# A decoder layer on one core: the first normalisation made a tile ahead and turned by VectorE in 32x32 squares, banks dealt anew, and a new order of the last attention step

## What is computed

```python
x = x + _L0_attn_ref(_layernorm(x, axis=-1), L0_attn_W_qkv, L0_attn_W_out, L0_attn_b_out)
x = x + _L0_xattn_ref(_layernorm(x, axis=-1), ctx_1024, ctx_1024, mask_Bx1xSxS2_ik1, ...)
x = x + _L0_ffn_ref(_layernorm(x, axis=-1), L0_ffn_w1, L0_ffn_b1, L0_ffn_w2, L0_ffn_b2)
```

## Time and profile before

| | us |
|---|---|
| median of 3 runs | 1269.24 |
| lowest, highest | 1269.16, 1270.24 |
| the profiled execution's own time | 1269.33 |
| its span, first to last instruction | 1266.9 |
| PE busy in the span | 1250.7 (99%) |
| DVE, ACT, POOL busy | 665.5, 487.4, 244.3 |

### The profile page before, as it was taken

The page is one execution under the profiler, slowest core; times in us unless marked ns, Lnnn a source line. Parts: engine busy times, 40 slices in busy tenths (PEclk is TensorE's granted clock), DMA queues, the critical chain, the costliest instruction groups (busy, mean ns, idle before and its releaser), DMA issues.

```text
span 1266.9 us, 15607 instructions
## 1 busy us (share of the span) xinstructions
PE 1250.7 (99%) x5785; PEld 1039.4 (82%) x5785; DVE 665.5 (53%) x1210; ACT 487.4 (38%) x887; POOL 244.3 (19%) x225
## 2 busy tenths in 40 slices
PE   9989999999999999999999999999999999999998
PEld 7878888888888888867888888888888888888887
DVE  7476858585858585856733443333424334433211
ACT  7246555545454545444332222322222322223221
POOL 2303232323232313138601002001001010020000
PEclk9999999999999999999999999999999999999999
DMA  8210202020202020316210010010100100100000
GB/s 294 81 63 13 76 14 75 13 75 12 75 12 75 12 75 12 125 40 210 75 67 1 1 67 1 1 66 0 36 30 0 66 0 0 66 0 0 34 1 34
DMA packets 40486, 60.04 MB, mean 47 GB/s; under 512 B 4224, under 2 KB 14464, under 8 KB 40448
## 3 DMA queue, kind: packets, MB, share of 16 engines
q1 hardware_dynamic: 40448, 59.53, 14.1%
HBM read 41.17 MB, written 18.35 MB: 47 GB/s over the span
## 4 chain that ended last, share of the span: by engine, by line
PE 54%; DMA 1%; SPq 0%; DVE 0%; ACT 0%; issue 0%; DVEq 0%
PE bank L50 18%; PE bank L52 18%; PE bank L51 18%; DMA w_raw<-in_w 0%; DMA x_dram<-resid 0%; DVE resid L1166 0%; SPq L1049 0%; DVE w_parts L185 0%; ACT w_parts L181 0%; SPq L1047 0%; SPq L189 0%; SPq L1046 0%; DVEq L1165 0%; SPq L1056 0%
## 5 line engine op out<-in xcount | busy, mean ns | idle before, releaser
L1156 DVE TENSOR_TENSOR hid_lo<-gelu_out,hid_hi 128x512 fp32r<-128x512 f32 x128 | 98.2, 767 | 399.1 <-ACT gelu_out L1123 399.0
L50 PE MATMUL bank<-zT,w_parts 128*128 128x512 f32 x768 | 299.3, 390 | 4.9 <-DVE zT L150 1.8
L52 PE MATMUL bank<-zT,w_parts 128*128 128x512 f32 x768 | 298.8, 389 | 0.0
L51 PE MATMUL bank<-zT,w_parts 128*128 128x512 f32 x768 | 298.8, 389 | 0.0
L1119 ACT ACTIVATE hid_hi<-bank,b_col 128x512 fp32r<-128x512 f32 x128 | 88.3, 690 | 491.0 <-PE bank L52 491.0
L50 PE MATMUL bank<-w2p_hi,hid_lo 128*128 128x512 f32 x512 | 199.3, 389 | 0.7 <-DVE hid_lo L1156 0.7
L52 PE MATMUL bank<-w2p_hi,hid_hi 128*128 128x512 f32 x512 | 199.2, 389 | 0.0
L51 PE MATMUL bank<-w2p_lo,hid_hi 128*128 128x512 f32 x512 | 199.2, 389 | 0.0
L50 PEld LDWEIGHTS bank<-zT,w_parts 128*128 128x128 f32 x768 | 144.2, 188 | 36.7 <-issue 3.0
L51 PEld LDWEIGHTS bank<-zT,w_parts 128*128 128x128 f32 x768 | 144.2, 188 | 29.8
L52 PEld LDWEIGHTS bank<-zT,w_parts 128*128 128x128 f32 x768 | 144.0, 188 | 29.9
(11 more groups left out here) (141 smaller groups left out, 1811.0 us busy)
## 6 DMA issues: line engine op xcount, KB each, us to landing
x_in<-in_x SPq DMA_DIRECT2D x32, 256.0 KB, 3.7
x_dram<-resid SPq DMA_DIRECT2D x32, 256.0 KB, 2.1
w_raw<-in_w SPq DMA_DIRECT2D x32, 256.0 KB, 3.4
resid<-x_dram SPq DMA_DIRECT2D x32, 256.0 KB, 3.1
out_dram<-resid SPq DMA_DIRECT2D x32, 256.0 KB, 2.1
resid<-in_wqkvT SPq DMA_DIRECT2D x12, 256.0 KB, 4.8
mask_i<-in_mask SPq DMA_DIRECT2D x16, 128.0 KB, 2.6
values_now<-values_dram SPq DMA_DIRECT2D x8, 256.0 KB, 2.8
```

Of the source, the lines that this page charges most:

```text
L50: pe.matmul(out_ap, lhs[1], rhs[0], start=start, stop=False)
L51: pe.matmul(out_ap, lhs[0], rhs[1], start=False, stop=False)
L52: return pe.matmul(out_ap, lhs[0], rhs[0], start=False, stop=stop)
L1156: dve.tensor_tensor(hid[1][:, c % 4, :], gelu_out[:, c % 2, :], f(hid[0][:, c % 4, :]), ALU.subtract).then_inc(hid_lo, 1)
```

## The change

**z1.** Rows of tile n are now loaded a second time into `ahead` (four buffers laid over `w1_raw` and `w2_raw`), their statistics are made in step n - 2, and in step n - 1 DVE makes the norm rows (`rows_ahead`) and turns them in 16 square transposes (`turn`) into the new `z1_cols`. ACT and DVE then split `z1_cols` into zT at the start of step n (`z1_high`, `z1_low`), as soon as the queries are done. PE's 16 transposes of z1 go from steps 1 to 7; the setup keeps those of tile 0. The norm rows of z1 leave the start of the step.

**Setup.** `load_ahead(1)` adds four transfers of 256 KB; DVE adds four statistics and their aggregation for tile 1 after its splits. The context values now wait in `z1_cols`, so in step 0 the first `turn` waits until they are stored.

**Banks and waits.** The tables are new; y goes to banks 0 to 3, and each chunk of it waits for `q_low` of its bank. The cross scores 0 to 3 wait for each `q_low` singly.

**Last step.** A new order of PE, ACT and DVE, the four `second_residual` of tile 7 moved into the feed-forward stage (before the second `w1_low` there), b1 and b2 loaded at the start of the attention block, and the gelu table loaded by a tiny activation in the last step.

The core of the diff:

```diff
                             if n == RAWS + NB - 1:
                                 for i in range(NB):
                                     load_x(sp, 0, i)
+                                load_ahead(sp, 1)
...
+                        stats_ahead(dve, 1, range(NB))
+                        aggregate(dve, 1, mv1, ln1)
                         dve.wait_ge(bias_loaded, 64)
...
+                        def rows_ahead(n, b):
+                            if b is not None:
+                                dve.wait_ge(z2T_done, NB * (b + 1))
+                            norm_rows(dve, lambda i: ahead[i], mv1, rstd1, ln1, n)
+                            dve.wait_ge(z1_ready, NB * (n + 1))
                             dve.nop(nofuse=True)
...
+                        def turn(a, first_turn, count):
+                            if more(a):
+                                for n in range(first_turn, first_turn + count):
+                                    dve.transpose(*squares(n, z1_cols)).then_inc(z1_turned, 1)
...
-                                for j in range(4):
+                                for j in range(3):
                                     mask_scores(b, j)
+                                if more(a):
+                                    rows_ahead(a + 1, b)
+                                mask_scores(b, 3)
+                            else:
+                                rows_ahead(1, None)
+                                dve.wait_ge(values_stored, 16 * BATCH)
+                                dve.nop(nofuse=True)
+                            turn(a, 0, 3)
                             for m in range(EC):
-                                low(yv, m, 4 + m, y_hi, y_lo, EC * a + m + 1)
-                            for i in range(NB):
+                                low(yv, m, m, y_hi, y_lo, EC * a + m + 1)
+                                if m == 2:
+                                    turn(a, 3, 2)
+                            turn(a, 5, 5)
+                            for i in range(NB):
+                                if i == 2:
+                                    turn(a, 10, 2)
...
+                            turn(a, 12, 2)
                             dve.wait_ge(s1_exp, NB * (a + 1))
...
+                            turn(a, 14, 2)
                             dve.wait_ge(pT_hi, a + 1)
...
-                                second_residual(b, 0, 1 - par)
-                                second_residual(b, 1, 1 - par)
-                                next_stats(dve, a + 1, (2, 3))
-                                second_residual(b, 2, 1 - par)
+                                second_residual(dve, b, 0, 1 - par)
+                                second_residual(dve, b, 1, 1 - par)
+                            if twice_more(a):
+                                stats_ahead(dve, a + 2, (2, 3))
+                                aggregate(dve, a + 2, mv1, ln1)
...
                             if b is not None:
                                 queries(b, range(EC))
-                                transposed_chunks(pe, a, 4)
...
-                            for i in range(NB):
-                                second_residual(b, i, b % 2, LAST_PROJ_BANK)
...
+                            act.wait_ge(b_loaded, 32)
+                            act.activation(gelu_table, b1_col[:, 0:1], ACT.Gelu)
...
+                            if splits_weights(t) and c == 0:
+                                for i in range(NB):
+                                    second_residual(dve, TILES - 1, i, (TILES - 1) % 2, LAST_PROJ_BANK)
```

More of the change, by code:

```diff
@@ L219, in decoder_layer_program @@
             values_stored, wo_lo = sem("values_stored"), sem("wo_lo")
-            values = [w2_raw[:, b, :] for b in range(STAGES)]
-            values.append(w1_raw[:, 0, :, :].rearrange("p c n -> p (c n)"))
+            z1_cols = sb("z1_cols", [P, EC, TILE])
+            values = [z1_cols[:, b, :] for b in range(BATCH)]
+            ahead = [w1_raw[:, i, :, :].rearrange("p c n -> p (c n)") for i in range(STAGES)]
+            ahead.append(w2_raw[:, 0, :])
+            ahead_loaded, z1_turned = [sem(f"ahead_loaded{i}") for i in range(NB)], sem("z1_turned")
             RAWS = 2 * NB
@@ L482, in first, with more, twice_more @@
                     return isinstance(t, int) and t == 0
+                def more(a):
+                    return not (isinstance(a, int) and a == TILES - 1)
+                def twice_more(a):
+                    return not (isinstance(a, int) and a >= TILES - 2)
                 with nc.Block() as block:
@@ L876, in queries @@
                             for m in chunks_:
-                                if m == 1 and not first(b):
-                                    pe.wait_ge(x2_ready, NB * b)
+                                if m < 2 and not first(b):
+                                    pe.wait_ge(x2_ready, NB * b - 2 + m)
                                 project(m, lambda c: at(wq, c, cols(m)), lambda c: at(zT, c), q_done)
```

255 lines of the change are left out of this document (156 added, 99 removed).

## The result

The changed kernel takes 1307.57 us (median of 5 runs, 1304.85 to 1309.02) against 1269.34 for the kernel before beside it: a ratio of 1.030, 95% interval 1.029 to 1.031, or +38.2 us where +24.6 was forecast. The direction was right, and so were the places of the two waits in each step; the time lies outside the forecast range.

What follows compares the result with a forecast made beforehand. PE was taken to bound the kernel. Steps 1 to 6 +25.8, step 7 -1.8, step 1 besides -1.4, setup +4.0, step 0 +3.2, last step and feed-forward -5.2: +24.6 on 1269.33, 1294 us; range 1272 to 1300.

Steps and rivals of the forecast that it cites:

- the two waits: Steps 1 to 6: PE waits about 1.3 us for the fourth masked pair and 3 to 4 for y's low parts.
- PE's transposes: Steps 1 to 7: removing PE's 16 transposes of z1, with the slower matmul behind them, saves 1.75 us a step.
- Norm rows 4.8 us beside GpSimd: Before the self scores: four norm rows meet GpSimd's silu parts and take 4.8 us, against 1.92 alone.
- no meeting: Rival, chance 0.20: norm rows do not meet GpSimd and take 1.9 us a step; 1277 us in all.
- faster: Rival, chance 0.09: the square transposes fit into VectorE's waits, so PE keeps its savings; 1258 us in all.
- The restarts behind waits: Steps 1 to 6: PE's restarts behind its new waits add 0.15 us a step.
- The tail: From self scores to the product of probabilities and values: eleven transposes on VectorE add 1.1 us of PE waiting a step.
- Setup +4.0: Before the first y: later weight chunks 2.5, tile 1's statistics 2.9, less 1.3 absorbed by a wait, make +4.0 us.
- Step 0, +3.2: Step 0: transposes ahead of the probabilities' low part add 1.5 us, statistics ahead of z2's low parts 1.7.
- step 1's -1.4: Step 1: PE's wait for the queries' low parts between cross scores goes, with its restarts, saving 1.4 us.
- Last step and feed-forward, -5.2: Last step and feed-forward start: 2 us of waits left of 7.3, saving 5.2 us (between 2 and 7).
- worse: Rival, chance 0.09: stalls push ACT and GpSimd out of step, another 1 to 2 us a step; 1303 us in all.

Runs made afterwards that it cites:

- pool_after_rows: Changed kernel with GpSimd's first low part of silu held until the four norm rows are made: 1299.42 us (one time).
- dose_before: Kernel before plus unused VectorE reductions (0.69 us each) between y's last two low parts, three in step 1, five or six in steps 2 to 7: 1275.25 us.
- pad_128: Kernel before with 128 unused bytes of each partition ahead of qo and later buffers: 1274.31 us (one time).
- pe_busy: Changed kernel with 12 useless matmuls (2.73 us) in TensorE's wait for y's low parts: 1317.18 us, ratio 1.037 to the kernel before.
- start_late: Changed kernel with setup and step 0 rearranged (tile 1's transfers behind the weights, its statistics in step 0, GpSimd's bias addition held): 1297.81 us (one time).
- rows_early: Changed kernel with the next tile's four norm rows made between the queries' low parts: 1281.86 us, ratio 1.009 to the kernel before.
- dose_after: Changed kernel with norm rows between the queries' low parts, plus up to six unused VectorE reductions a step ahead of y's last low part: 1292.16 us.
- best3: best2 with VectorE's steps written out in place of a loop and the small tile 256 bytes in place of 128: 1253.24 us, ratio 0.987 to the kernel before.
- best2: Changed kernel with norm rows moved earlier, start rearranged, square transposes dealt into VectorE's waits: 1259.63 us, ratio 0.991 to the kernel before.

## Why the prediction was wrong, step by step

- **PE's transposes, -1.75 a step: right.** Step 7, which has no new work, gained 1.46, that is 1.7 less the 0.25 of the slower output matmuls.
- **Norm rows 4.8 us beside GpSimd: right** (4.87), and shown by pool_after_rows to be GpSimd's doing. The working behind the 4.8 was loose: three rows that each wait for one part of GpSimd would make 1.92 + 3 x 1.27 = 5.7, but a row and a part take only 1.48 us side by side. So the number is better than its reason. The square transposes at 0.70 and the two waits (1.3 and 3 to 4 forecast, 1.35 and 3.17 found) were right too. The rivals "no meeting" and "faster" fall with them.
- **The restarts behind waits, 0.15 a step: this step failed.** It prices what comes behind a wait at the full clock, whatever the length of the wait, and has no term for the clock. The trace that it read has waits up to 1.84 us, all without a fall; dose_before and pad_128 show that this was the luck of that execution. Behind waits of 3 us the slower matmuls cost: 1.6 in y of step 0, 1.6 in its product, 2.5 in the queries of step 1, 2.7 in its scores, and 1.67 in the scores of each step 2 to 6. pe_busy shows the cause for the self scores. For the first three the granted clock is low in the trace, but no run fills those waits; start_late, which shortened all three, had y and the product back at 11.00 and 2.86 but not the queries.
- **The tail, +1.1 a step: right in size, wrong in sum.** It is there in rows_early and pe_busy (1.05 in rows_early). Two delays that end at the same VectorE are not to be added: with slow scores the tail's waits vanish, and the clock costs a steady step 1.67 - 1.1, or 0.48 by pe_busy.
- **A missing term: addresses.** 0.25 us a step and 0.28 a feed-forward tile, 3.7 us in all. The forecast costed instructions and never the bytes by which a new tile shifts the others. pad_128 shows it.
- **Setup +4.0: 3.2.** The chunks came later as said (VectorE splits them at 21.66, before 19.88), but that cost 1.75 us and not 2.5: VectorE ends its splits at 40.5 in place of 38.8. The statistics took 2.9, as forecast.
- **Step 0, +3.2, and step 1's -1.4:** the parts without the clock are +3.2 (two waits of 3.2 and 3.4 us in place of 1.6 and 1.8), and the rest is the clock. In step 1 the wait for the queries' low parts went, as forecast.
- **Last step and feed-forward, -5.2: mis-sized.** The last step won 2.2 and the first feed-forward tile 2.05 (87.46 for 89.51), 4.2 in all; the other seven tiles lost 0.28 each.

The sum: the forecast's 24.6, the clock in steps 0 and 1 (8.4, less 1.1 of tail), the clock over the tail in steps 2 to 6 (0.6 x 5 = 2.9), addresses 3.7 and 1.0 less won at the end, less 0.8 in the setup, gives 38.7 against 38.9 in the spans. The rival "worse" at 1303 had the nearest time and another reason: it had ACT and GpSimd pushed out of step, and in steps 1 to 7 of the changed kernel PE waits for neither.

## What to carry to other kernels

Moving work from a full engine to a half idle one is a matter of where, not of how much: the same sixteen transposes and four rows cost 3% when they stood ahead of what TensorE waited for, and, with the new start and the addresses mended, won 1.3% once each stood in a wait of VectorE that the trace shows and VectorE's loop was written out. Look first for the partner: an instruction that lies beside GpSimd's may take two and a half times as long there and its usual time a few microseconds earlier. Where a forecast has TensorE wait for two or three microseconds, give the clock a term of its own, with a chance, since the same wait came with and without a fall here, and price it against the slack of the engine that is due next. And after adding a small tile, compare the pitch of matmuls that did not change.

## What the hardware showed that was not expected

- TensorE's granted clock fell to its lower level in the matmuls behind waits of 1.8 to 3.4 us, and these took 1.3 to 3.2 us longer. The length of the wait does not settle it: of the waits ahead of the self scores 1.81 us came without a fall and 1.91 with one, and 2.98 again without; a wait of 3.05 us ahead of the first y came with one in the changed kernel (12.62 us for 48 matmuls) and without in dose_after (10.99); in pool_after_rows equal waits of 3.18 us were followed by scores of 5.32 and 6.87 us. The wait of 1.84 us ahead of the queries of step 1 came with a fall in five traces and without in four; two of the five and three of the four are the kernel before or a copy of it with doses or unused bytes.
- 128 bytes more of each partition ahead of other tiles made unchanged matmuls slower: 36 output matmuls 8.39 us in place of 8.17, a feed-forward tile 87.32 in place of 87.04; 2048 bytes did not. best3's 2304 for qo and w2p and 256 for hid had the feed-forward tile at 87.04 again, and the output matmuls nearly so (8.16 to 8.24).
- VectorE paused 3.03 us where its loop turned back in the one profiled execution of best2, and not where the steps were written out (best3, which changed the addresses too; no run changes the loop alone); PE paused 2.97 and 2.75 us in its feed-forward loop in the profiled execution of pe_busy alone.
- GpSimd stretched the norm rows also in step 0 of the changed kernel: 5.88 us for four beside its bias additions, 1.92 in start_late, where these were held back.
